# Second attention on 64-row pairs over doubled stacks, with its maxima closed one unit later and its stacks filled by four transfers

## What is computed

```python
B, S = (1, 256); HEAD_DIM = DIM // NUM_HEADS          # 512 // 32 = 16
q = (query @ Wq).reshape(b, sq, NUM_HEADS, HEAD_DIM).transpose(0, 2, 1, 3)
k = (key @ Wk).reshape(b, sk, NUM_KV_HEADS, HEAD_DIM).transpose(0, 2, 1, 3)
v = (value @ Wv).reshape(b, sk, NUM_KV_HEADS, HEAD_DIM).transpose(0, 2, 1, 3)
k = jnp.repeat(k, rep, axis=1); v = jnp.repeat(v, rep, axis=1)     # 8 KV heads, rep = 4
probs = jax.nn.softmax(jnp.einsum('bhqd,bhkd->bhqk', q, k) * HEAD_DIM ** (-0.5), axis=-1)
out = jnp.einsum('bhqk,bhkd->bhqd', probs, v) ... @ Wo
```

## Time and profile before

| | |
|---|---|
| median of three executions | 1120.84 us |
| the profiled execution | 1123.95 us |
| its span | 1122.1 us |
| PE, DVE, ACT, POOL busy | 91%, 59%, 43%, 33% of the span |
| attention of layer 1, first scores to last product with V | 912 to 1055 us from the span's start |

### The profile page before, as it was taken

How to read it: one execution, slowest core, us unless ns; L and a number is a source line. 1 busy time by engine, 2 the same in 40 slices (tenths; PEclk the granted TensorE clock), 3 DMA queues, 4 the chain that set the end, 5 groups by cost and what they waited for, 6 DMA issues and landing times. The chain is left out here.

```text
span 1122.1 us, 18616 instructions
## 1 busy us (share of the span) xinstructions
PE 1019.9 (91%) x6780; PEld 880.7 (78%) x6780; DVE 658.2 (59%) x1128; ACT 484.6 (43%) x943; POOL 371.4 (33%) x252
## 2 busy tenths in 40 slices
PE   5899999999999999999999999998998579999964
PEld 4888989889798898988989889896777357777543
DVE  5475566457456546745745664673475546667396
ACT  4365346336435534733643563461231125555311
POOL 4207305503620830560363074041891300000054
PEclk9999999999999999999999999998998689999986
DMA  6002001100200200110020021000621183121000
GB/s 206 1 1 95 1 1 56 37 0 5 88 0 0 93 0 0 56 37 0 0 93 0 0 61 51 0 1 1 197 76 38 38 205 63 30 56 30 1 1 37
DMA packets 29617, 46.49 MB, mean 41 GB/s; under 512 B 3216, under 2 KB 12048, under 8 KB 29584
## 3 DMA queue, kind: packets, MB, share of 16 engines
q1 hardware_dynamic: 29008, 46.03, 13.8%
q10 hardware_dynamic: 576, 0.00, 0.0%
HBM read 41.83 MB, written 4.19 MB: 41 GB/s over the span
## 5 line engine op out<-in xcount | busy, mean ns | idle before, releaser
L430 DVE TENSOR_TENSOR ptL<-tbank,ptH 128x512 fp32r<-128x512 f32 x192 | 132.2, 688 | 84.4 <-ACT ptH L290 84.3
L290 ACT ACTIVATE ptH<-tbank 128x512 fp32r<-128x512 f32 x192 | 115.8, 603 | 109.4 <-PE tbank L539 109.1
L205 POOL TENSOR_TENSOR oTL<-o_norm,oTH 128x512 fp32r<-128x512 f32 x32 | 41.3, 1291 | 350.4 <-ACT oTH L310 350.4
L539 PE MATMUL tbank<-ident,probs 128*128 128x128 f32 x864 | 132.2, 276 | 16.6 <-DVE ptL L430 12.2
L443 DVE TENSOR_REDUCE negmax<-score 128x1 f32<-128x768 f32 x128 | 119.5, 948 | 19.7 <-PE score L74 19.7
L401 DVE TENSOR_REDUCE sumsq<-probs 128x2 f32<-128x256 f32 (+1 forms) x80 | 42.1, 526 | 136.9 <-ACT probs L285 71.8
L316 ACT ACTIVATE probs<-score,negmax 128x768 f32<-128x768 f32 x128 | 115.6, 903 | 15.5 <-DVE negmax L443 15.5
L72 PE MATMUL obank<-ptH,vH 128*128 128x256 f32 x384 | 122.2, 318 | 0.0
L539 PEld LDWEIGHTS tbank<-ident,probs 128*128 128x128 f32 x864 | 98.3, 140 | 26.5 <-DVE ptL L430 15.1
L74 PE MATMUL score<-wkvH,kvT_lo 128*128 128x256 f32 x384 | 108.7, 283 | 0.0
L73 PE MATMUL score<-wkvL,kvT_hi 128*128 128x256 f32 x384 | 108.7, 283 | 0.0
(11 more groups left out here) (252 smaller groups left out, 2469.3 us busy)
## 6 DMA issues: line engine op xcount, KB each, us to landing
wqo_stage<-in_wq SPq DMA_DIRECT2D x9, 1024.0 KB, 5.7
wqo_stage<-in_wo SPq DMA_DIRECT2D x8, 1024.0 KB, 5.2
wkv_stage<-in_wkv SPq DMA_DIRECT2D x9, 512.0 KB, 6.5
a_qS<-q_scratch SPq DMA_DIRECT2D x32, 128.0 KB, 3.8
ctx_stage<-in_ctxT SPq DMA_DIRECT2D x2, 1024.0 KB, 13.6
kS<-k_scratch SPq DMA_DIRECT2D x32, 64.0 KB, 2.2
q_scratch<-part SPq DMA_DIRECT2D x8, 256.0 KB, 4.1
wqo_stage<-in_down_w SPq DMA_DIRECT2D x3, 512.0 KB, 4.6
```

The source lines that it names most:

```text
L290: act.activation(out, tbank[c % 2][:], ACT.Copy, scale=scale).then_inc(t_hi, 1)
L430: i = dve.tensor_tensor(out, tbank[c % 2][:], f32(hi), ALU.subtract)
L539: i = pe.transpose(tbank[c % 2][:, n * P:(n + 1) * P], block_in, S.ident[:])
```

## The change

`kS` and `qS` hold the 64-row stack twice, in rows 0 to 63 and in rows 64 to 127, and the two memsets and their semaphore waits go. `q_dram` is laid out by KV head, high or low, width and (head, row). A transfer now fills 32 rows, in `load_k` both parts at once and in `load_q` one part twice, by a broadcast over a leading axis of 2. A query tile is stored by four transfers of 64 rows instead of two of 128.

On PE every product of scores and transposed scores contracts over 64 rows, one of a pair over the lower half (`low`) and one over the upper (`high`), into different banks. The maxima of a unit are added by eight products of 64 rows and 128 columns instead of four of 128 rows and 256 columns: four right behind the transposed scores (`begin_maxima`), and four in the next step, ahead of the next transposed scores (`finish_maxima`), which alone releases the exponential. `negmax` has four buffers instead of two. `times_v`, the transposes and `finish_quad` move back: `times_v` from `v % 4 == 1` to 2, the transposes from 2 to 3, `finish_quad` from 3 to 0 of the next quad.

```diff
@@ ffn0 @@
             sp.wait_ge(S.k_out, 64)
-            sp.wait_ge(k_zeroed, 1)
             for s in range(2):
                 S.load_k(sp, s, s)
...
-            pool.memset(f32(S.kS[64:P, :, :]), 0.0).then_inc(k_zeroed, 1)
-            pool.wait_ge(k_zeroed, 1)
@@ attn1 @@
-    negmax = sb("a_negmax", [P, 4], f32r)
+    MB = 4
+    negmax = sb("a_negmax", [P, 2 * MB], f32r)
-    q_dram = nc.dram_tensor("q_scratch", (2, HID, ROWS), fp32, kind="Internal").ap()
+    q_dram = nc.dram_tensor("q_scratch", (KVH, 2, D1, GRP * ROWS), fp32, kind="Internal").ap()
+    H = P // 2
+    low, high = slice(0, H), slice(H, P)
@@ SP @@
-            sp.wait_ge(zeroed, 2)
             def load_q(g, s):
-                for n in range(4):
-                    heads = q_dram[n // 2].rearrange("(h d) n -> d h n", d=D1)
-                    sp.dma_start(f32(qS[D1 * n:D1 * (n + 1), s, :, :]),
-                                 heads[:, bass.ds(g * GRP, GRP), :]).then_inc(stack_in[s], 16)
+                for c in range(4):
+                    sp.dma_start(f32(qS[32 * c:32 * (c + 1), s, :, :].rearrange("p h n -> p (h n)")),
+                                 q_dram[bass.ds(g, 1), c % 2].to_broadcast([2, D1, GRP * ROWS])).then_inc(stack_in[s], 16)
             for t in range(NQ):
                 sp.wait_ge(q_lo, t + 1)
                 for r in range(2):
-                    sp.dma_start(q_dram[r, t * P:(t + 1) * P, :], f32(part[t % 2][:, r, :])).then_inc(q_out[t % 2], 16)
+                    for i in range(2):
+                        sp.dma_start(q_dram[2 * t + i, r].rearrange("d (h n) -> h d n", h=GRP),
+                                     f32(part[t % 2][i * H:(i + 1) * H, r, :])).then_inc(q_out[t % 2], 16)
                 if t == 0:
-                    sp.wait_ge(q_out[0], 32)
+                    sp.wait_ge(q_out[0], 64)
                     load_q(0, 0)
                     load_q(1, 1)
@@ POOL @@
-            pool.memset(f32(qS[64:P, :, :, :]), 0.0).then_inc(zeroed, 1)
-            pool.wait_ge(zeroed, 2)
@@ PE @@
-                    q = b * SQ + t * P
-                    pe.matmul(score[t][:], qS[:, s, j, q:q + P], kS[:, s, b * SC:(b + 1) * SC],
+                    q, rows = b * SQ + t * P, (low, high)[t]
+                    pe.matmul(score[t][:], qS[rows, s, j, q:q + P], kS[rows, s, b * SC:(b + 1) * SC],
                               start=True, stop=True).then_inc(pe_s, 1)
+            def add_maxima(v, order, stop):
+                for t in range(2):
+                    m = negmax[:, 2 * (v % MB) + t:2 * (v % MB) + t + 1]
+                    for half, rows in enumerate((low, high)):
+                        bank = scoreT[v % 2][:, 512 * order[half]:512 * (order[half] + 1)]
+                        q = t * P + H * half
+                        x = pe.matmul(bank.rearrange("p (k q) -> p k q", k=2)[:, :, q:q + H],
+                                      m[rows].to_broadcast([H, P]), ident_r[rows, rows].unsqueeze(1).to_broadcast([H, 2, H]),
+                                      start=False, stop=stop and t == 1)
+                return x
@@ scores_T @@
+                for k in range(2):
+                    for half, rows in enumerate((low, high)):
+                        key = b * SC + (2 * half + k) * P
+                        pe.matmul(scoreT[v % 2][:, 512 * half + k * SQ:512 * half + (k + 1) * SQ], kS[rows, s, key:key + P],
+                                  qS[rows, s, j, b * SQ:(b + 1) * SQ], start=k == 0, stop=False)
+            def begin_maxima(n, v):
+                pe.wait_ge(s_max, 2 * n + 2)
+                add_maxima(v, (0, 1), False).then_inc(pe_m, 1)
+            def finish_maxima(n, v):
+                pe.wait_ge(pe_m, n + 1)
+                add_maxima(v, (1, 0), True).then_inc(pe_sT, 1)
@@ turn of PE @@
+                    if not first or v >= 1:
+                        finish_maxima(n - 1, (v - 1) % NU)
                     scores_T(n, v, first)
+                    begin_maxima(n, v)
                     if not first or v >= GRP:
-                        if v % GRP == 1:
+                        if v % GRP == 2:
                             times_v(r - 1, (v // GRP - 1) % QUADS, i if v >= GRP else i - 1, first)
-                        if v % GRP == 2:
+                        if v % GRP == 3:
                             transpose_o(r - 1, (v // GRP - 1) % 2)
@@ load_k @@
-                for n in range(4):
-                    sp.dma_start(f32(S.kS[D1 * n:D1 * (n + 1), s, :]),
-                                 S.k_dram[n % 2, bass.ds(g * D1, D1), :]).then_inc(S.stack_in[s], 16)
+                for c in range(4):
+                    sp.dma_start(f32(S.kS[32 * c:32 * (c + 1), s, :]),
+                                 S.k_dram[:, bass.ds(g * D1, D1), :]).then_inc(S.stack_in[s], 16)
```

More of the change, by code:

```diff
@@ L691, in ffn0 @@
     pe_v, v_done = sem("pe_v"), sem("v_rows_done")
-    k_zeroed, stats3_done = sem("k_zeroed"), sem("stats3_done")
+    stats3_done = sem("stats3_done")
     w_in = {n: sem(f"{n}_in") for n in ("gate", "affine")}
@@ L1246, in attn1 @@
     win = sem("a_win")
-    pe_s, s_max, ident_set = sem("a_pe_s"), sem("a_s_max"), sem("a_ident_set")
+    pe_s, pe_m, s_max, ident_set = sem("a_pe_s"), sem("a_pe_m"), sem("a_s_max"), sem("a_ident_set")
     pe_sT, s_exp, pe_pv = (sem(f"a_{n}") for n in ("pe_sT", "s_exp", "pe_pv"))
@@ L1297, in _ @@
             for stored in q_out:
-                sp.wait_ge(stored, 32 * NQ // 2)
+                sp.wait_ge(stored, 64 * NQ // 2)
             ffn.loads(sp)
@@ L1324, in _ @@
                 if t >= 2:
-                    act.wait_ge(q_out[t % 2], 32)
+                    act.wait_ge(q_out[t % 2], 64)
                 act.activation(part[t % 2][:, 0, :], halves[t], ACT.Copy, scale=float(D1) ** -0.5).then_inc(q_hi, 1)
@@ L1370, in maxima @@
                     dve.wait_ge(pe_s, 2 * n + t + 1)
-                    dve.tensor_reduce(negmax[:, 2 * (v % 2) + t:2 * (v % 2) + t + 1], score[t][:], AX.X, ALU.max,
+                    dve.tensor_reduce(negmax[:, 2 * (v % MB) + t:2 * (v % MB) + t + 1], score[t][:], AX.X, ALU.max,
                                       negate=True).then_inc(s_max, 1)
@@ L1378, in turn @@
                         maxima(n + 1, (v + 1) % NU)
-                    if v % GRP == 3 and (not first or v >= GRP):
-                        finish_quad(i, r - 1, v // GRP - 1)
+                    if v % GRP == 0 and (not first or v >= 2 * GRP):
+                        finish_quad(i, r - 2, v // GRP - 2)
                     if v == 4 and not first:
@@ L1404, in _ @@
             turns(dve, turn)
-            finish_quad(TURNS - 1, QUADS * TURNS - 1, QUADS - 1)
+            for w in (QUADS - 2, QUADS - 1):
+                finish_quad(TURNS - 1, QUADS * (TURNS - 1) + w, w)
             def add_out(t):
@@ L1445, in scores_T @@
                     pe.wait_ge(s_exp, n - 1)
-                pe.wait_ge(s_max, 2 * n + 2)
[L1447 to L1457, removed]
+                for k in range(2):
[4 more added lines that the diff above has]
+            def begin_maxima(n, v):
+                pe.wait_ge(s_max, 2 * n + 2)
+                add_maxima(v, (0, 1), False).then_inc(pe_m, 1)
+            def finish_maxima(n, v):
+                pe.wait_ge(pe_m, n + 1)
+                add_maxima(v, (1, 0), True).then_inc(pe_sT, 1)
             def times_v(r, w, i, first):
@@ L1495, in _ @@
             turns(pe, turn)
+            finish_maxima(NU * TURNS - 1, NU - 1)
             times_v(QUADS * TURNS - 1, QUADS - 1, TURNS - 1, False)
```

## The result

The changed kernel takes 1284.01 us (median of 4 runs, 1280.72 to 1287.49), the kernel before 1120.07 beside it (4 runs): ratio 1.1461, 95% interval 1.1416 to 1.1505, 164 us slower. The profiled execution is the one of 1280.72 us, with a span of 1278.6.

What follows compares the result with a forecast made beforehand. PE, busy for 91%, bound the kernel before; afterwards two-engine fills would. First scores at 956, six refills and the tail gave span 1270, +148 us; 1123.95 plus 148 is 1272, less 3.1 for the median 1269 us, range 1232 to 1345.

Steps and rivals of the forecast that it cites:

- The deciding step: Attention's stack fills: outermost axis 2 leaves two DMA engines, 50.6 GB/s, 31.1 us a fill instead of under 8; chance 0.81.
- side-by-side pairs: PE's products over disjoint 64-row halves: a pair costs as much as one product, 0.90 us a unit instead of 1.38.
- `ffn0`: First `load_k` over two engines delays the weight piece behind it, so POOL ends later: +4.4 us (0 to 12).
- The memset: Layer norm without the qS memset: PE's wait of 2.62 us goes, -2.6 us.
- Start of the attention: Stores over 4 engines and two query loads put the first scores at 956 instead of 912.25, +44 us.
- First refill: In the attention, it goes out 18.2 us after the first scores, as before, at 974.4.
- Five periods: Attention refills strictly one after another, 35.1 us each; the last of six lands at 1183.
- Tail: After the last refill lands, 21 us to L1503 at 1204, then an unchanged 66.0 to the end.
- The quad of 7.5 us: Four attention units without stack waits: 3 x 1.43 + (0.90 + 1.93 + 0.41), 15 us less over 16 quads.
- rival 2: All 16 engines, pairs one after another: PE pays 0.42 us a unit, 1145 us, up to 1158; chance 0.03.
- Rival 1: All 16 engines carry the fills, pairs side by side: a fill of 9.1 us, nothing waits, 1103 us; chance 0.11.
- Rival 3: Two engines at the slow row's rate, 20.4 GB/s: a fill of 77 us, about 1600 us; above 1345 chance 0.05.

Runs made afterwards that it cites:

- kernel 8: experiment 6 with the key fills also by eight transfers of 16 rows, so that query and key rows match; 1114.4 us, ratio 0.9953.
- Experiment 1: The changed kernel with only the row order of the fills turned, outermost axis 16, same bytes and number of transfers; 1135.97 us, ratio 1.0136.
- experiment 5: Experiment 1 with DVE's low half of a weight split one step later in the last turn; 1124.66 us, ratio 1.0075.
- experiment 6: experiment 5 with query scratch and stores as before, query fills of 16 rows, second stack filled behind tile 1's stores; rows paired wrongly; 1110.79 us.
- kernel 7: experiment 6 with `times_v` split into two groups of 16 products, on either side of the next unit's scores; 1120.97 us, ratio 1.0046.

## Why the prediction was right, and where it was off

**The deciding step**, two engines a fill, held, and so did the side-by-side pairs: 1284.0 against 1269, within the range. The share of 0.13, the six waits 36.6 us apart, the wait of ACT's copy (47 us, said 45) and POOL's (21.9, said 15 to 18) are the marks that it had named; the share of 1.0 that would have refuted it is not there. Of the 15 us between the medians, 8.7 are between the profiled execution (1280.72) and the 1272 said for it; 3.3 are its distance from the median after, and 3.1 what the step took off for the median before. Step by step, where the profiled span of 1278.6 differs from 1270:

- **Ahead of `ffn0`**: that execution reached it 7.4 us earlier (its first product in this trace at 777.09, in the one before at 784.46), without a part of the change in it. -7.4. Over the ten traces this point lies anywhere from 776.6 to 784.5, so this is luck: in the parts that the change touches the step was 16.0 us short, not 8.6.
- **`ffn0`**: from that product to the attention's first transposes 106.6 us (777.09 to 883.71), before 99.1: +7.5, said +4.4. In kernel 8 the same stretch takes 99.0, so the two-engine fill is the whole of it. Priced too low: POOL waited 21.9 us for the piece, not 15 to 18. The step left out that SP's eight issues ahead of the piece would themselves take longer, 7.0 us instead of 3.6; the piece then landed 18.9 us after its issue instead of 3.8. +3.1.
- **The memset**: the gap of 2.62 us is gone, as said; all sixteen transposes stand together at 883.71. It was worth more than 2.6: from the first transposes to the first store are 9.3 us (883.71 to 892.99), before 14.3 (883.54 to 897.87), as the projections behind it ran at a higher clock too (granted 0.77 from 890 to 900 before, 1.00 from 892 to 897 after). -2.5, which is part of the next line.
- **Start of the attention**: transposes to scores 67.3 us (883.71 to 951.00); the step made it 956 - (883.54 + 4.4) = 68.1. -0.8. It is made of a store over 4 engines (5.2 + 2; the chain shows 7.07 behind the last of four issues), two fills and the stores queued behind. That it fits so well is partly luck: the -2.5 of the memset hides +1.7 behind the first store, most of it the stretch from there to the first fill (8.97 us, said 7.3).
- **First refill**: 20.7 us behind the first scores (971.68 - 951.00), said 18.2. +2.5.
- **Five periods**: 183.1 us, said 175.5. +7.6, the largest error. The transfer was sized well (issue to scores 32.7, said 33.1); the 2 us for units and SP's issue were 3.8. The granted clock in these stretches was 0.67 and 0.73 of the full 2.4 GHz, a mean of its two levels (half is 1.2), and between a landing and the next issue it was the lower one: 0.50 from 1004 to 1008, where the scores at 1004.37 take 0.79 us.
- **Tail**: from the last fill's scores (1187.45) to L1520, which was L1503, 25.1 us (to 1212.57), said 21. +4.1: the granted clock was 0.51 from 1187 to 1195, for which the step had 1 us, and the quad behind it at full clock took 8.6 us, not 7.5. From there to the end 66.0, as before.

With the last fill half a microsecond shorter (-0.5) these sum to +8.6, the difference.

**The quad of 7.5 us** was wrong, though in the likeliest case little hung on it. The step took ACT's loop of 1.43 us as the limit of three units and added `times_v` to a fourth. Experiment 1 shows 8.04: DVE is busy for 5.8 us a quad and then waits 2.2 us, since the scores it needs stand behind `times_v`. The four units were each priced, but not DVE's sum over the quad beside PE's longest uninterrupted stretch. The step also misread a row: the 0.41 us behind `times_v` are idle time of the weight loads (PEld), not of PE. PE's next product starts at 969.55, 1.86 us after the start of `times_v` at 967.69, so 1.93 + 0.41 counts 0.48 us too much, and without that error the step would have given 7.1, further from 8.04. The 13 us that rival 2 adds for 0.41 at both sides of the transposes rest on the same reading.

**Rival 1**, at 1103 us, was priced 33 us too low even when its condition is met. Three costs were missing. The ring with the weight splits in the last turn is 10.8 us by the traces (experiment 5); the sentence on the four-buffer maxima had put the later release at nothing. The start of the attention takes 36.9 us where this case allowed 28.7 - 2.6 = 26.1, 10.8 more; the stores over four engines are shown for 6.3 of it, and their form, the doubled first fills and the order of the second share the rest (experiment 6). The quads are 16 x 0.54 = 8.6 us. Together 30.2; the last 3 us are not taken apart, though the first quads ran at half clock. So the sentence that these parts "lie beside this and cost nothing" was right only where PE waited for transfers anyway. It hid a cost that would have become visible the moment the transfers were mended.

**Rival 2**, pairs one after another, is ruled out by the two products of a pair starting 0.003 us apart, and by four of them in 0.17 us. **Rival 3**, slower engines, by 26.5 GB/s each.

## What to carry to other kernels

Before a transfer is merged with others or given a broadcast, look at its outermost axis on both sides: here the axis order alone, with the same bytes and the same number of transfers, was worth 148 us. When a saving in products is weighed, sum each engine over the whole cycle of the schedule and add the stretch in which it must wait for another's longest block; and when a release is moved one step later, follow it through the stages where other work shares the engines, as the last turn did here.

## What the runs showed of the hardware that was not expected

- **SP is held by slow transfers.** The eight issues of the first query fills took 14.68 us in the changed kernel and the eight stores behind them 28.5; they took 5.11 and 7.4 us in kernel 1, where the fills ran over 16 engines and the stores over the same 4.
- **A few-engine fill delays what stands behind it.** The weight piece issued behind the two-engine key fills landed 18.9 us after its issue, where it took 3.8 before, and its reader waited 21.9 us instead of 3.50. It fits that the piece is as late as its part on the two busy engines; the views here don't tell the engines apart.
- **Idle weight loads are not idle PE.** The 0.41 us behind `times_v` belong to the weight loads. PE's last four products of 32 output rows start at 969.22 and its next product, of 128, at 969.55, 0.33 us later, where two groups of four within `times_v` are 0.22 apart. So this change of tile shape shows 0.11 us on PE, not 0.41; kernel 7 shows the same 0.33 (991.97 to 992.30), from 32 output rows to products of 64 rows.
- **The clock after a pause.** In kernel 1 the clock was at 0.50 of full from 912 to 930, behind a wait in which PE did nothing (0.00 us busy from 900 to 912), 0.82 in the same stretch before. The first quad behind it takes 9.7 us (932.38 to 942.05) instead of 8.0; that is part of why a late start costs more than its own length:

```profile
912.00:930.00 18.00, 11.43 (x78) 10.15 (x80) 9.55 (x17) 4.84 (x6) 0.00 (x0) 0.50 0.32 110
```
